# Pairwise bilinear interaction on one core: a quarter of the products summed over elements by VectorE in place of TensorE

## The chip, the core and the metric

One core of one Trainium2 chip. The metric is the device time of one execution in microseconds (us); the time before is the median of 3 runs. TensorE is called PE, VectorE DVE, ScalarE ACT, GpSimd POOL, SyncE SP.

## What is computed

2048 samples, 32 fields, embeddings of 64 floats (fp32 throughout). For every sample and each of the 496 pairs of fields a bilinear form with its own 64 x 64 matrix, then three dense layers:

```python
e = jnp.stack([tbl_0[ids[:, 0]], ..., tbl_31[ids[:, 31]]], axis=1)        # (2048, 32, 64)
row_idx, col_idx = np.triu_indices(32, k=1)
z = jnp.einsum('bpe,fpe,bpf->bp', e[:, row_idx], kernel, e[:, col_idx])   # (2048, 496)
h = jnp.concatenate([z, dense_ctx], axis=1)                               # (2048, 512)
h = jnp.maximum(h @ W_top1 + b_top1, 0.0)                                 # 512
h = jnp.maximum(h @ W_top2 + b_top2, 0.0)                                 # 256
y = h @ W_top3                                                            # 1
```

## The kernel before, in words

The samples go through in 4 chunks of 512. A chunk's embeddings are gathered by POOL (L202), one indirect DMA per field and 128 samples, 8 for a pair of fields, into a ring of 4 pairs. A "turn" on PE (L238) transposes a pair's rows into `side_ps`, so that elements lie in partitions and samples in columns; ACT copies it to `xt` (L363), a ring of 24 pairs: field 2q in partitions 0 to 63, field 2q+1 in 64 to 127.

The unit of work is the duo: for the field pairs s < q all four products of their fields. Its matmuls (L312, L313, each two instructions in fp32) have the kernel matrices as weights and the samples of pair q moving, half the rows of the array each, side by side, into one of 3 two-bank tiles `y_ps`. Four "special" duos a chunk hold the pairs inside field pairs (L315 to L318). DVE multiplies the 128 x 1024 result by x of pair s (L461) into one of 6 `products`. What is left is the sum over the 64 elements, which lie in partitions: PE does it by matmuls with a selector (L330), 4 column groups side by side, for two duos (a quad) at a time, collecting 16 quads in `sum_ps` before ACT copies the bank to `z_sb`. 124 duos and 62 quads make a chunk. The results of four banks, with 16 dense values put into the last by four DMAs, are the input of the dense layers ("layer1" four jobs, "layer2" two, "layer3" one; L250, L257, L264).

Turns and dense layers are side jobs: they share the one tile `side_ps`, so each waits until ACT has taken the one before. The order is written out by hand in `side_schedule`: the duos come in the order of q, after each duo number d with d % 4 == 1 the sums of the two quads before the last two duos, and side jobs just after such sums; the dense layers of a chunk run within the next one, and four times a chunk two jobs stand at one place. The last chunk's tower runs at the end (`last_tower`). The waits that pace PE and DVE:

```python
pe.wait_ge(duo_multiplied, g - Y_RING + 1)                # before the matmuls of duo g
pe.wait_ge(duo_multiplied, 2 * g + 2)                     # before the sum of quad g
dve.wait_ge(quad_summed, (g - PRODUCT_RING) // 2 + 1)     # before the multiply of duo g
```

Of the kernel before, what the change touches and what calls it, by code (L numbers as in the profile page):

```python
# [7 lines left out]
ALU = mybir.AluOpType  # L8
# [4 lines left out]
P = 128  # L13
# [4 lines left out]
ROW_RING = 4  # L18
XT_RING = 24
Y_RING = 3  # L20
PRODUCT_RING = 6
SPECIALS = PAIRS // 4


def duo_list():
# [12 lines left out]
DUO = duo_list()  # L38
DUOS = len(DUO)
QUADS = DUOS // 2  # L40
FIRST_DUO = {q: DUO.index(("block", 0, q)) for q in range(1, PAIRS)}
SPECIAL_DUO = {u: DUO.index(("special", u, None)) for u in range(SPECIALS)}

Z_QUADS = P // 8
Z_BANKS = -(-QUADS // Z_QUADS)
SUM_ROWS = 2 * (QUADS - (Z_BANKS - 1) * Z_QUADS)

PIECES = [(0, 4)] + [(d, d + 8) for d in range(4, DUOS, 8)]
# [14 lines left out]
def z_rows():  # L63
    rows, dense = [], 0
    for kb in range(Z_BANKS):
        for r in range(P):
            column_tile, s, half = r // 32, r % 32 // 2, r % 2
            quad = kb * Z_QUADS + s
            if quad < QUADS:
                duo = DUO[2 * quad + column_tile // 2]  # L70
                rows.append(tuple(sorted(field_pair(duo, column_tile % 2, half))))
            else:
                rows.append(dense)
                dense += 1
    return rows


def quads_after(d):


    return (d // 2 - 2, d // 2 - 1) if d % 4 == 1 else ()


def after_sums(d):

    return d - (d - 2) % 4


def side_schedule():

    before = {(c, d): [] for c in range(CHUNKS) for d in range(DUOS)}
    for c in range(CHUNKS):
        for q in range(PAIRS):
            if c == 0:
                at = 0 if q < 2 else FIRST_DUO[q] if q < 7 else after_sums(min(FIRST_DUO[q] - 4, 30 + 6 * (q - 8)))
                before[0, at].append(("turn", 0, q))
            elif q < 8:
                before[c - 1, after_sums(82 + 6 * q if c == 1 else 66 + 7 * q)].append(("turn", c, q))
            else:
                before[c, after_sums(6 + 7 * (q - 8))].append(("turn", c, q))  # L100
    for c in range(CHUNKS - 1):
        for n in range(4):
            before[c + 1, after_sums(10 + 6 * n)].append(("layer1", c, n))
        for n in range(2):
            before[c + 1, after_sums(38 + 8 * n)].append(("layer2", c, n))
        before[c + 1, after_sums(60)].append(("layer3", c, 0))
    after = [("layer1", CHUNKS - 1, n) for n in range(4)] + [("layer2", CHUNKS - 1, n) for n in range(2)]
    after.append(("layer3", CHUNKS - 1, 0))
    return before, after


SIDE_BEFORE, SIDE_AFTER = side_schedule()
SIDE_ORDER = [job for c in range(CHUNKS) for d in range(DUOS) for job in SIDE_BEFORE[c, d]] + SIDE_AFTER
# [3 lines left out]
def dlrm_tower(nc, ids, tables, pair_kernel, dense, w1, b1, w2, b2, w3, out):  # L117
    with ExitStack() as ctx:
# [9 lines left out]
        kernel_sb = sb("kernel_sb", [P, DUOS, 2 * E])  # L128
        xt = sb("xt", [P, XT_RING, N])
        special = sb("special", [P, 2, 2, N])  # L130
        rows = sb("rows", [P, ROW_RING, TILES, 2, E])
        products = sb("products", [P, PRODUCT_RING, 2, N])
        z_sb = sb("z_sb", [P, Z_BANKS, N])
# [7 lines left out]
        y_sb = sb("y_sb", [P, N])  # L141
# [8 lines left out]
        ids_landed = [sem(f"ids_landed{i}") for i in range(2)]  # L150
        rows_landed = [sem(f"rows_landed{i}") for i in range(ROW_RING)]
# [10 lines left out]
        duo_ready = sem("duo_ready")  # L162
        duo_multiplied = sem("duo_multiplied")
        quad_summed = sem("quad_summed")
        bank_kept = sem("bank_kept")
        out_written = sem("out_written")

        LAST_BANK = Z_BANKS - 1

        def x_of(c, q):  # L170
            return xt[:, (c * PAIRS + q) % XT_RING]

# [13 lines left out]
        def _(pool):  # L186
# [4 lines left out]
            for c in range(CHUNKS):  # L191
                if c < 2:
                    pool.wait_ge(ids_landed[c], 16)
                for q in range(PAIRS):
                    slot = q % ROW_RING
                    if c or q >= ROW_RING:
                        before = c * PAIRS + q - ROW_RING
                        pool.wait_ge(side_ready, SIDE["turn", before // PAIRS, before % PAIRS] + 1)
                    for h in range(2):
                        j = 2 * q + h  # L200
                        for t in range(TILES):
                            pool.indirect_dma_start(rows[:, slot, t, h, :], None, tables[j],  # L202
                                                    bass.IndirectOffsetOnAxis(ap=idx[:, c, t, j:j + 1], axis=0)
                                                    ).then_inc(rows_landed[slot], 16)

        @block.sync
        def _(sp):
# [8 lines left out]
            def place_dense(c):  # L216
                for g in range(4):
                    sp.dma_start(z_sb[32 * g + SUM_ROWS:32 * g + 32, LAST_BANK, :],
                                 dense[4 * g:4 * g + 4, c * N:c * N + N]).then_inc(dense_landed[c], 16)

            place_dense(0)
            for c in range(CHUNKS):
                if c + 1 < CHUNKS:
                    sp.wait_ge(side_ready, SIDE["layer1", c, 3] + 1)
                    place_dense(c + 1)
                sp.wait_ge(side_kept, SIDE["layer3", c, 0] + 1)
                sp.dma_start(out[:, c * N:c * N + N], y_sb[32 * c:32 * c + 1, :]).then_inc(out_written, 16)
# [3 lines left out]
        def _(pe):  # L231
            def turn(c, q):
                k = SIDE["turn", c, q]
                pe.wait_ge(rows_landed[q % ROW_RING], (c * (PAIRS // ROW_RING) + q // ROW_RING + 1) * 2 * TILES * 16)
                if k:
                    pe.wait_ge(side_kept, k)
                for t in range(TILES):
                    last = nc.tensor.transpose(side_ps[:, t * P:(t + 1) * P],  # L238
                                               rows[:, q % ROW_RING, t].rearrange("p h e -> p (h e)"), identity[:])
                last.then_inc(side_ready, 1)  # L240

            def layer1(c, n):
                if n == 0:
                    pe.wait_ge(bank_kept, banks_kept(c, LAST_BANK))
                    pe.wait_ge(dense_landed[c], 4 * 16)
# [3 lines left out]
                for kb in range(4):  # L249
                    last = nc.tensor.matmul(tower_bank(c, 1, n), w1_sb[:, kb, n * P:n * P + P], z_sb[:, kb, :],  # L250
# [17 lines left out]
            def last_tower(c):  # L268
                pe.wait_ge(side_kept, SIDE["layer1", c, 0])
                pe.wait_ge(bank_kept, banks_kept(c, LAST_BANK - 1))  # L270
                for n in range(4):
                    for kb in range(LAST_BANK):
                        nc.tensor.matmul(tower_bank(c, 1, n), w1_sb[:, kb, n * P:n * P + P], z_sb[:, kb, :],  # L273
                                         start=(kb == 0), stop=False)
                pe.wait_ge(bank_kept, banks_kept(c, LAST_BANK))
                pe.wait_ge(dense_landed[c], 4 * 16)
                for n in range(4):
                    nc.tensor.matmul(tower_bank(c, 1, n), w1_sb[:, LAST_BANK, n * P:n * P + P], z_sb[:, LAST_BANK, :],  # L278
# [14 lines left out]
            def side(job):  # L293
                kind, c, n = job
                if kind == "turn":
                    turn(c, n)
                elif kind == "layer1":
# [6 lines left out]
            def bilinear(c, d):  # L304
                g = c * DUOS + d
                if g >= Y_RING:
                    pe.wait_ge(duo_multiplied, g - Y_RING + 1)
                kind, s, q = DUO[d]
                y = y_ps[g % Y_RING]
                low, high = slice(0, E), slice(E, P)  # L310
                if kind == "block":
                    nc.tensor.matmul(y[:, 0, :], kernel_sb[low, d, :], x_of(c, q)[low, :], start=True, stop=True)  # L312
                    last = nc.tensor.matmul(y[:, 1, :], kernel_sb[high, d, :], x_of(c, q)[high, :], start=True, stop=True)  # L313
                else:
                    nc.tensor.matmul(y[low, 0, :], kernel_sb[low, d, low], x_of(c, 4 * s + 3)[low, :], start=True, stop=True)  # L315
                    nc.tensor.matmul(y[low, 1, :], kernel_sb[high, d, low], x_of(c, 4 * s)[high, :], start=True, stop=True)  # L316
                    nc.tensor.matmul(y[high, 0, :], kernel_sb[low, d, high], x_of(c, 4 * s + 2)[low, :], start=True, stop=True)  # L317
                    last = nc.tensor.matmul(y[high, 1, :], kernel_sb[high, d, high], x_of(c, 4 * s + 1)[high, :],  # L318
                                            start=True, stop=True)
                last.then_inc(duo_ready, 1)  # L320

            def add_up(c, quad):
                g = c * QUADS + quad
                pe.wait_ge(duo_multiplied, 2 * g + 2)
                kb, s = quad // Z_QUADS, quad % Z_QUADS
                if s == 0 and c * Z_BANKS + kb >= 1:
                    free = c * Z_BANKS + kb - 1
                    pe.wait_ge(bank_kept, banks_kept(free // Z_BANKS, free % Z_BANKS))
                for m in range(4):
                    last = nc.tensor.matmul(sum_ps[32 * m:32 * m + 32, :], selector[:, 30 - 2 * s:62 - 2 * s],  # L330
                                            products[:, (2 * g + m // 2) % PRODUCT_RING, m % 2, :],
                                            start=(s == 0), stop=(s == Z_QUADS - 1 or quad == QUADS - 1))
# [4 lines left out]
            for c in range(CHUNKS):  # L337
                stored, pieces = 0, 0
                for d in range(DUOS):
                    for job in SIDE_BEFORE[c, d]:  # L340
                        side(job)
                    kind, s, q = DUO[d]
                    need = SIDE["turn", c, q if kind == "block" else 4 * s + 3] + 1
                    if need > stored:
                        stored = need
                        pe.wait_ge(side_kept, stored)
                    if c == 0 and pieces < len(PIECES) and PIECES[pieces][0] == d:
                        pe.wait_ge(kernel_landed[pieces], 16)
                        pieces += 1
                    bilinear(c, d)  # L350
                    for quad in quads_after(d):
                        if quad >= 0:
                            add_up(c, quad)
                        elif c:
                            add_up(c - 1, QUADS + quad)
# [5 lines left out]
        def _(act):  # L361
# [3 lines left out]
            def store(c, q):  # L365
                k = SIDE["turn", c, q]
                if c * PAIRS + q >= XT_RING:
                    act.wait_ge(duo_multiplied, ((c * PAIRS + q - XT_RING) // PAIRS + 1) * DUOS)
# [17 lines left out]
            def keep3(c):  # L386
                k = SIDE["layer3", c, 0]
                act.wait_ge(side_ready, k + 1)
                copy(y_sb[32 * c:32 * c + 32, :], tower_bank(c, 3, 0)[32 * c:32 * c + 32, :]).then_inc(side_kept, 1)

            def keep(job):
                kind, c, n = job
                if kind == "turn":
                    store(c, n)
                elif kind == "layer1":
# [6 lines left out]
            def special_slots(c, u):  # L402
                n = c * SPECIALS + u
                if n >= 2:
# [102 lines left out]
```

## Time and profile before

| | |
|---|---|
| median of 3 runs | 896.94 us (896.54 to 897.68) |
| profiled execution: its time / its span | 896.94 / 894.2 us |
| PE busy | 831.9 us (93%) |
| DVE busy | 574.1 us (64%), 499 instructions |
| ACT busy | 114.3 us (13%) |
| POOL busy | 484.1 us (54%) |
| mean granted PE clock | 0.989 of full speed |

Busy times are of one profiled execution; PE's weight loads, which run beside its matmuls, are kept apart. In a row of the timeline "x8" merges neighbouring instructions of one kind; the time in brackets is the idle time of the engine before it and what ended it.

### The profile page before, as it was taken

Reading aid. Unit: us, or ns where it says so; the run is one execution under the profiler, and the core shown is the slowest. Engines: PE = TensorE matmul, PEld = TensorE weight load, DVE = VectorE, ACT = ScalarE, POOL = GpSimd, SP = SyncE. Lnnn points to the kernel's source line nnn. Section 1 sums busy time; section 2 is a strip of 40 time slices with the busy share of each in tenths; the row PEclk is TensorE's granted clock in tenths of the full one; section 3 lists DMA queues with packets and bytes.
Section 4 is the critical chain, followed back from the end, with each engine's and each line's share of the span. In section 5 each row is a group of like instructions: output and inputs, shape, how many; then the busy total and the mean of one; then the engine's idle time right before and its main releaser. Section 6 shows DMA issues by size and latency. Waiting matters only on the chain.

```text
span 894.2 us, 10971 instructions
## 1 busy us (share of the span) xinstructions
PE 831.9 (93%) x4496; PEld 293.4 (33%) x4496; DVE 574.1 (64%) x499; ACT 114.3 (13%) x185; POOL 484.1 (54%) x518
## 2 busy tenths in 40 slices
PE   0377999999899999999999999999999999999999
PEld 0122333333333333333333333333333333333323
DVE  0144778778666566787785466787775664788870
ACT  0011010100121011102111110200120210100112
POOL 6777777777777777477735555377746330000000
PEclk9988999999999999999999999999999999999999
DMA  9411111111111111011101111011111000000000
GB/s 340 156 27 26 28 27 27 27 28 27 26 27 26 29 28 26 17 27 26 27 13 21 21 19 22 13 28 25 27 18 22 14 14 1 1 1 1 1 1 0
DMA packets 19881, 27.64 MB, mean 31 GB/s; under 512 B 9012, under 2 KB 9268, under 8 KB 19704
## 3 DMA queue, kind: packets, MB, share of 16 engines
q0 software_dynamic: 16384, 16.81, 10.4%
q1 hardware_dynamic: 3448, 10.14, 3.1%
q8 instruction: 35, 0.57, 0.3%
q14 instruction: 14, 0.11, 0.0%
HBM read 26.91 MB, written 0.01 MB: 30 GB/s over the span
## 4 chain that ended last, share of the span: by engine, by line
PE 69%; POOL 22%; issue 7%; ACT 1%; DMA 0%; DVEq 0%; DVE 0%; ACTq 0%; POOLq 0%
PE y_ps L312 35%; POOL rows L202 22%; PE sum_ps L330 19%; PE side_ps L250 5%; PE side_ps L238 3%; PE side_ps L257 2%; PE y_ps L315 1%; PE y_ps L273 1%; ACT xt L363 1%; PE y_ps L283 1%; PE y_ps L313 1%; PE side_ps L264 1%; PE y_ps L278 0%; DMA rows<-tbl_dram,idx 0%; DMA idx<-ids_dram 0%
## 5 line engine op out<-in xcount | busy, mean ns | idle before, releaser
L461 DVE TENSOR_TENSOR products<-y_ps,xt 128x1024 f32<-128x1024 f32 x480 | 556.3, 1217 | 287.2 <-PE y_ps L313 287.0
L202 POOL DMA_INDIRECT rows<-tbl_dram,idx x512 | 483.4, 944 | 239.7 <-issue 151.7
L312 PE MATMUL y_ps<-xt,kernel_sb 64*128 64x512 f32 x960 | 459.0, 616 | 4.1 <-ACT xt L363 4.1
L313 PE MATMUL y_ps<-xt,kernel_sb 64*128 64x512 f32 x960 | 459.2, 617 | 0.0
L312 PEld LDWEIGHTS y_ps<-xt,kernel_sb 64*128 64x128 f32 x960 | 168.6, 190 | 256.7 <-issue 145.0
L330 PE MATMUL sum_ps<-products,selector 128*32 128x512 f32 x1984 | 238.8, 598 | 0.7 <-DVE products L461 0.7
L313 PEld LDWEIGHTS y_ps<-xt,kernel_sb 64*128 64x128 f32 x960 | 168.6, 190 | 0.0
L330 PEld LDWEIGHTS sum_ps<-products,selector 128*32 128x32 f32 x1984 | 51.6, 109 | 170.4 <-DVE products L461 94.2
L363 ACT ACTIVATE xt<-side_ps 128x512 f32<-128x512 f32 x64 | 38.2, 598 | 442.9 <-PE side_ps L238 442.8
L238 PE MATMUL side_ps<-identity,rows 128*128 128x128 f32 x256 | 44.2, 298 | 46.1 <-DMA rows<-tbl_dram,idx 46.1
L238 PEld LDWEIGHTS side_ps<-identity,rows 128*128 128x128 f32 x256 | 28.3, 146 | 100.2 <-issue 60.1
L250 PE MATMUL side_ps<-z_sb,w_sb 128*128 128x512 f32 x96 | 44.3, 604 | 4.8 <-ACT xt L363 4.8
L363 ACT ACTIVATE z_sb<-sum_ps 28x512 f32<-28x512 f32 (+1 forms) x28 | 16.6, 592 | 208.3 <-PE sum_ps L330 208.0
L363 ACT ACTIVATE special<-xt 64x512 f32<-64x512 f32 x64 | 40.1, 627 | 1.6
L250 PEld LDWEIGHTS side_ps<-z_sb,w_sb 128*128 128x128 f32 x96 | 17.2, 189 | 28.3 <-issue 25.4
L257 PE MATMUL side_ps<-h_sb,w_sb 128*128 128x512 f32 x48 | 22.2, 605 | 4.5 <-ACT xt L363 4.5
L461 DVE TENSOR_TENSOR products<-y_ps,special 128x1024 f32<-128x1024 f32 x16 | 19.5, 1217 | 6.0 <-issue 4.3
L377 ACT ACTIVATE h_sb<-side_ps,b_sb 128x512 f32<-128x512 f32 x12 | 8.2, 687 | 73.6 <-PE side_ps L250 73.6
L317 PE MATMUL y_ps<-xt,kernel_sb 64*64 64x512 f32 x32 | 17.1, 615 | 0.0
L315 PE MATMUL y_ps<-xt,kernel_sb 64*64 64x512 f32 x32 | 17.1, 615 | 0.0
L316 PE MATMUL y_ps<-xt,kernel_sb 64*64 64x512 f32 x32 | 17.1, 614 | 0.0
L318 PE MATMUL y_ps<-xt,kernel_sb 64*64 64x512 f32 x32 | 17.1, 614 | 0.0
(29 smaller groups left out, 73.1 us busy)
## 6 DMA issues: line engine op xcount, KB each, us to landing
rows<-tbl_dram,idx POOLq DMA_INDIRECT x512, 2.4
kernel_sb<-pair_kernel_dram SPq DMA_DIRECT2D x15, 512.0 KB, 11.1
w_sb<-w_dram SPq DMA_DIRECT2D x1, 1024.0 KB, 18.2
w_sb<-w_dram SPq DMA_DIRECT2D x1, 512.0 KB, 17.5
kernel_sb<-pair_kernel_dram SPq DMA_DIRECT2D x1, 256.0 KB, 2.8
z_sb<-dense_dram SPq DMA_DIRECT2D x16, 8.0 KB
idx<-ids_dram SPq DMA_DIRECT2D x1, 192.0 KB, 6.9
idx<-ids_dram SPq DMA_DIRECT2D x1, 64.0 KB, 1.9
```

Source lines behind the costliest of these rows:

```text
L202: pool.indirect_dma_start(rows[:, slot, t, h, :], None, tables[j], bass.IndirectOffsetOnAxis(ap=idx[:, c, t, j:j + 1], axis=0)).then_inc(r ...
L238: last = nc.tensor.transpose(side_ps[:, t * P:(t + 1) * P], rows[:, q % ROW_RING, t].rearrange("p h e -> p (h e)"), identity[:])
L250: last = nc.tensor.matmul(tower_bank(c, 1, n), w1_sb[:, kb, n * P:n * P + P], z_sb[:, kb, :], start=(kb == 0), stop=(kb == 3))
L257: last = nc.tensor.matmul(tower_bank(c, 2, n), w2_sb[:, kb, n * P:n * P + P], h1_sb[:, kb, :], start=(kb == 0), stop=(kb == 3))
L312: nc.tensor.matmul(y[:, 0, :], kernel_sb[low, d, :], x_of(c, q)[low, :], start=True, stop=True)
L313: last = nc.tensor.matmul(y[:, 1, :], kernel_sb[high, d, :], x_of(c, q)[high, :], start=True, stop=True)
L315: nc.tensor.matmul(y[low, 0, :], kernel_sb[low, d, low], x_of(c, 4 * s + 3)[low, :], start=True, stop=True)
L316: nc.tensor.matmul(y[low, 1, :], kernel_sb[high, d, low], x_of(c, 4 * s)[high, :], start=True, stop=True)
L317: nc.tensor.matmul(y[high, 0, :], kernel_sb[low, d, high], x_of(c, 4 * s + 2)[low, :], start=True, stop=True)
L330: last = nc.tensor.matmul(sum_ps[32 * m:32 * m + 32, :], selector[:, 30 - 2 * s:62 - 2 * s], products[:, (2 * g + m // 2) % PRODUCT_RING, ...
L363: return nc.scalar.activation(dst, src, ACT.Copy)
L461: nc.vector.tensor_tensor(products[:, g % PRODUCT_RING], y_ps[g % Y_RING][:], by, ALU.mult).then_inc(duo_multiplied, 1)
```

## The change

Of the 124 duos, the 28 with s < 4 and q in (4, 6, 8, 9, 10, 12, 13) are replaced by 28 batches. A batch (q, t) takes 128 samples of pair q as weights and the kernel matrices of the four duos (s = 0 to 3) moving: its result has samples in partitions and, for both fields of pair q, 8 x 64 elements in columns. DVE multiplies it by the gathered rows of fields 0 to 7, which are kept untransposed (`kept_rows`, two chunks deep), into one of 2 `batch_products`, and after the multiply of the next unit adds up the 64 elements of each group in one `tensor_reduce` (1024 elements to 16 per partition). The 16 results go to `z_batch`, to which dense is now loaded with one DMA; one more turn per chunk ("turn_batch") makes it the fourth bank `z_turned`. Duos and batches are units: 96 duos, 28 batches, 48 quads a chunk, three banks. Sums come after the second duo of four as before, or after the batch that follows it. Side jobs may stand before the sums of a place (odd keys) or after them (even keys), one at each place. `PRODUCT_RING` goes from 6 to 5, `special` from two buffers to one, the ring of gathered rows to 3.

The order in chunks 1 to 3 as it comes out (d duo, s special duo, b batch, S two quads' sums, T a turn, TB the batch turn, L1, L2, L3 layer jobs; a line ends at its sums):

```
dd TB S          T5 dddd L1 S       sdbddb T6 S        T7 ddbddb L1 S
ddbddb L1 S      T8 ddbdsb S        T9 ddddb L1 S      T10 ddddb S
L2 ddbddb S      T11 ddddb L2 S     ddbddb L3 S        ddddb S
T12 ddsdb S      ddbddb S           T13 ddddb S        ddbddb S
T14 ddddb S      ddddb S            ddbddb S           ddddb S
T15 ddbdd S      dddd S             T0 ddsd T1 S       T2 dddd T3 S, T4 dd
```

T0 to T4 on the last lines are of the next chunk, and chunk 3 has there only TB, before the sums of "ddsd". In chunk 0 there are no L jobs; from T10 on its order is: T10 ddddb, ddbddb, T11 ddddb, ddbddb, ddddb, T12 ddsdb, ddbddb and on as above.

```diff
-PRODUCT_RING = 6
+PRODUCT_RING = 5
+BATCH_RING = 2
+BATCH_Q = (4, 6, 8, 9, 10, 12, 13)
...
+        units.append(duo)
+        due = BATCHES * (a // 4 + 1) // (DUOS // 4 - 4)
+        if a % 2 and waiting and placed < due:
+            units.append(waiting.pop(0))
...
+    places = [key for g in range(CHUNKS * UNITS - 1) if SUMS_AFTER[g] for key in (2 * g + 1, 2 * g + 2)]
...
             def bilinear(c, p):
-                    pe.wait_ge(duo_multiplied, g - Y_RING + 1)
+                    pe.wait_ge(unit_multiplied, g - Y_RING + 1)
...
+                else:
+                    d, samples = PLACE["block", 0, s], slice(q * P, q * P + P)
+                    nc.tensor.matmul(y[:, 0, :], x_of(c, s)[low, samples],
+                                     kernel_sb[low, d:d + KEPT, :].rearrange("p d f -> p (d f)"), start=True, stop=True)
+                    last = nc.tensor.matmul(y[:, 1, :], x_of(c, s)[high, samples],
+                                            kernel_sb[high, d:d + KEPT, :].rearrange("p d f -> p (d f)"),
+                                            start=True, stop=True)
...
+                bilinear(c, p)
+                for job in SIDE_AT[2 * g + 1]:
+                    side(job)
+                for of, quad in SUMS_AFTER[g]:
+                    add_up(of, quad)
...
+            def sum_batch(n):
...
+                dve.wait_ge(unit_multiplied, batch_unit(n) + 1)
+                nc.vector.tensor_reduce(z_batch[:, t, 16 * block:16 * block + 16],
+                                        batch_products[:, n % BATCH_RING].rearrange("p b i e -> p (b i) e"),
+                                        mybir.AxisListType.X, ALU.add).then_inc(batch_summed, 1)
...
+                dve.wait_ge(unit_ready, g + 1)
+                if kind == "batch":
+                    if batches >= BATCH_RING:
+                        dve.wait_ge(batch_summed, batches - BATCH_RING + 1)
+                    by = kept_rows[:, c % 2, q].rearrange("p i e -> p (i e)").unsqueeze(1).to_broadcast([P, 2, N])
...
+                    if duos >= PRODUCT_RING:
+                        dve.wait_ge(quad_summed, (duos - PRODUCT_RING) // 2 + 1)
...
+                nc.vector.tensor_tensor(into, y[:], by, ALU.mult).then_inc(unit_multiplied, 1)
+                if p and UNIT[p - 1][0] == "batch":
+                    sum_batch(batches - 1)
```

## Rows read from the trace of the kernel before

**Rows 1.** The page, busy us of each engine, share of the span, instructions.
```profile
PE 831.9 (93%) x4496; PEld 293.4 (33%) x4496; DVE 574.1 (64%) x499; ACT 114.3 (13%) x185; POOL 484.1 (54%) x518
```
**Rows 2.** The page, costliest groups: line, engine, form, count | busy us, mean ns | idle before.
```profile
L461 DVE TENSOR_TENSOR products<-y_ps,xt 128x1024 f32<-128x1024 f32 x480 | 556.3, 1217 | 287.2 <-PE y_ps L313 287.0
...
L312 PE MATMUL y_ps<-xt,kernel_sb 64*128 64x512 f32 x960 | 459.0, 616 | 4.1 <-ACT xt L363 4.1
...
L330 PE MATMUL sum_ps<-products,selector 128*32 128x512 f32 x1984 | 238.8, 598 | 0.7 <-DVE products L461 0.7
```
**Rows 3.** The chain that ended last, a layer 1 job in two chunks: start, us.
```profile
473.04 3.67 PE side_ps L250 x8
...
680.55 3.67 PE side_ps L250 x8
```
**Rows 4.** Timeline of PE in chunk 3: start us, us, instruction.
```profile
807.53 1.92 PE L330 MATMUL sum_ps<-products,selector 128*32 128x512 f32 x16
809.39 0.69 PE L312 MATMUL y_ps<-xt,kernel_sb 64*128 64x512 f32 x1
...
810.35 0.59 PE L312 MATMUL y_ps<-xt,kernel_sb 64*128 64x512 f32 x1
...
812.07 0.59 PE L312 MATMUL y_ps<-xt,kernel_sb 64*128 64x512 f32 x1
...
813.02 1.92 PE L330 MATMUL sum_ps<-products,selector 128*32 128x512 f32 x16
```
**Rows 5.** Timeline of DVE over the same stretch.
```profile
806.25 3.48 DVE L461 TENSOR_TENSOR products<-y_ps,xt 128x1024 f32<-128x1024 f32 x3
810.63 4.62 DVE L461 TENSOR_TENSOR products<-y_ps,xt 128x1024 f32<-128x1024 f32 x4 [0.91 <-PE y_ps L313]
```
**Rows 6.** Timeline of PE, sums and the side jobs between them.
```profile
264.03 0.66 PE L238 MATMUL side_ps<-identity,rows 128*128 128x128 f32 x4 [0.40 <-DMA rows<-tbl_dram,idx]
...
265.53 3.67 PE L250 MATMUL side_ps<-z_sb,w_sb 128*128 128x512 f32 x8 [0.84 <-ACT xt L363]
...
272.76 1.92 PE L330 MATMUL sum_ps<-products,selector 128*32 128x512 f32 x16
...
281.88 1.92 PE L330 MATMUL sum_ps<-products,selector 128*32 128x512 f32 x16
...
357.46 1.92 PE L330 MATMUL sum_ps<-products,selector 128*32 128x512 f32 x16
...
364.65 1.93 PE L330 MATMUL sum_ps<-products,selector 128*32 128x512 f32 x16
...
388.13 1.92 PE L330 MATMUL sum_ps<-products,selector 128*32 128x512 f32 x16
...
394.25 1.92 PE L330 MATMUL sum_ps<-products,selector 128*32 128x512 f32 x16
```
**Rows 7.** Timeline of PE, turns that waited for rows, first sum of chunk 1.
```profile
84.15 0.66 PE L238 MATMUL side_ps<-identity,rows 128*128 128x128 f32 x4 [3.90 <-DMA rows<-tbl_dram,idx]
...
244.07 0.66 PE L238 MATMUL side_ps<-identity,rows 128*128 128x128 f32 x4 [1.92 <-DMA rows<-tbl_dram,idx]
...
249.98 1.93 PE L330 MATMUL sum_ps<-products,selector 128*32 128x512 f32 x16
```
**Rows 8.** Timeline of PE and DVE, the last sums.
```profile
862.78 1.93 PE L330 MATMUL sum_ps<-products,selector 128*32 128x512 f32 x16
...
865.88 2.36 DVE L461 TENSOR_TENSOR products<-y_ps,xt 128x1024 f32<-128x1024 f32 x2 [0.87 <-PE y_ps L313]
...
866.55 1.06 PE L330 MATMUL sum_ps<-products,selector 128*32 128x512 f32 x8
...
868.29 1.06 PE L330 MATMUL sum_ps<-products,selector 128*32 128x512 f32 x8 [0.67 <-DVE products L461]
```
**Rows 9.** Stretches: us, busy us (count) of PE, PEld, DVE, ACT, POOL, PE clock, DMA share, GB/s.
```profile
80.00:100.00 20.00, 16.11 (x86) 6.28 (x84) 10.10 (x10) 3.71 (x6) 15.12 (x17) 0.91 0.15 27
100.00:150.00 50.00, 50.00 (x302) 17.46 (x302) 39.90 (x36) 6.06 (x10) 37.82 (x41) 1.00 0.16 27
```

More of the change, by code:

```diff
@@ L63, in z_rows @@
 def z_rows():
-    rows, dense = [], 0
+    rows = []
     for kb in range(Z_BANKS):
@@ L67, in z_rows @@
             column_tile, s, half = r // 32, r % 32 // 2, r % 2
[L68 to L71, printed above, removed]
-            else:
[L73 to L100, printed above, removed]
+            duo = DUO[2 * (kb * Z_QUADS + s) + column_tile // 2]
@@ new lines, in z_rows, with sum_schedule @@
+            rows.append(tuple(sorted(field_pair(duo, column_tile % 2, half))))
+    for q in BATCH_Q:
+        rows += [(i, 2 * q + bank) for bank in range(2) for i in range(2 * KEPT)]
+    return rows + list(range(DENSE))
+def sum_schedule():
+    after, summed = {g: [] for g in range(CHUNKS * UNITS)}, 0
+    waits = [FIRST_UNIT[q] - 1 for q in range(2, 8)]
+    for c in range(CHUNKS):
+        for p in range(UNITS):
+            duos = sum(at <= p for at in DUO_AT)
+            upto = summed
+            if c == 0 and p in waits:
+                upto = duos // 2
+            elif duos % 4 == 2 and (p == UNITS - 1 or UNIT[p + 1][0] != "batch"):
+                upto = c * QUADS + duos // 2 - 1
+            after[c * UNITS + p] = [divmod(quad, QUADS) for quad in range(summed, upto)]
+            summed = max(summed, upto)
+    return after
@@ new lines, with side_schedule @@
+SUMS_AFTER = sum_schedule()
+def side_schedule():
+    at = {key: [] for key in range(2 * CHUNKS * UNITS)}
+    places = [key for g in range(CHUNKS * UNITS - 1) if SUMS_AFTER[g] for key in (2 * g + 1, 2 * g + 2)]
+    for c in range(CHUNKS):
+        after = (c + 1) * UNITS if c < CHUNKS - 1 else c * UNITS + LAST_BATCH + 8
+        at[min(key for key in places if key > 2 * after)].append(("turn_batch", c, 0))
+    later = 2 * CHUNKS * UNITS
+    for c in reversed(range(CHUNKS)):
+        for q in reversed(range(PAIRS)):
+            if c == 0 and q < 8:
+                key = 2 * FIRST_UNIT[q] if q else 0
+            else:
+                last = 2 * (c * UNITS + FIRST_UNIT[max(q, 1)] - 2)
+                key = later = max(key for key in places if key <= last and key < later and not at[key])
+            at[key].insert(0, ("turn", c, q))
@@ L101, in side_schedule @@
     for c in range(CHUNKS - 1):
+        free = [key for key in places if key > 2 * (c + 1) * UNITS + 8 and not at[key]]
         for n in range(4):
-            before[c + 1, after_sums(10 + 6 * n)].append(("layer1", c, n))
+            at[free[2 * n]].append(("layer1", c, n))
         for n in range(2):
-            before[c + 1, after_sums(38 + 8 * n)].append(("layer2", c, n))
-        before[c + 1, after_sums(60)].append(("layer3", c, 0))
+            at[free[8 + 2 * n]].append(("layer2", c, n))
@@ L107, in side_schedule @@
+        at[free[12]].append(("layer3", c, 0))
     after = [("layer1", CHUNKS - 1, n) for n in range(4)] + [("layer2", CHUNKS - 1, n) for n in range(2)]
     after.append(("layer3", CHUNKS - 1, 0))
-    return before, after
-SIDE_BEFORE, SIDE_AFTER = side_schedule()
-SIDE_ORDER = [job for c in range(CHUNKS) for d in range(DUOS) for job in SIDE_BEFORE[c, d]] + SIDE_AFTER
+    return at, after
+SIDE_AT, SIDE_AFTER = side_schedule()
+SIDE_ORDER = [job for key in range(2 * CHUNKS * UNITS) for job in SIDE_AT[key]] + SIDE_AFTER
@@ L150, in dlrm_tower @@
         ids_landed = [sem(f"ids_landed{i}") for i in range(2)]
+        kept_landed = [sem(f"kept_landed{q}") for q in range(KEPT)]
         rows_landed = [sem(f"rows_landed{i}") for i in range(ROW_RING)]
@@ L336, in _ @@
             pe.wait_ge(selector_made, 2)
[L337 to L355, printed above, removed]
+            stored, pieces = 0, 0
+            for g in range(CHUNKS * UNITS):
+                c, p = divmod(g, UNITS)
+                for job in SIDE_AT[2 * g]:
+                    side(job)
+                need = SIDE["turn", c, top_pair(UNIT[p])] + 1
+                if need > stored:
+                    stored = need
+                    pe.wait_ge(side_kept, stored)
+                kind, s, q = UNIT[p]
+                place = PLACE["block", 0, s] + KEPT - 1 if kind == "batch" else PLACE[UNIT[p]]
+                while c == 0 and pieces < len(PIECES) and PIECES[pieces][0] <= place:
+                    pe.wait_ge(kernel_landed[pieces], 16)
+                    pieces += 1
+                bilinear(c, p)
+                for job in SIDE_AT[2 * g + 1]:
+                    side(job)
+                for of, quad in SUMS_AFTER[g]:
+                    add_up(of, quad)
             add_up(CHUNKS - 1, QUADS - 2)
@@ L414, in copy_bank @@
+                copy(special[high, 0, :], x_of(c, 4 * u + 2)[high, :]).then_inc(special_kept, 1)
+                copy(special[low, 0, :], x_of(c, 4 * u + 3)[high, :]).then_inc(special_kept, 1)
             def copy_bank(c, kb):
-                act.wait_ge(quad_summed, c * QUADS + min(Z_QUADS * (kb + 1), QUADS))
-                if c and kb == 0:
+                act.wait_ge(quad_summed, c * QUADS + Z_QUADS * (kb + 1))
+                if c and kb == 1:
                     act.wait_ge(side_ready, SIDE["layer1", c - 1, 3] + 1)
-                if kb < LAST_BANK:
-                    copy(z_sb[:, kb, :], sum_ps[:]).then_inc(bank_kept, 1)
-                else:
-                    for g in range(4):
-                        part = slice(32 * g, 32 * g + SUM_ROWS)
-                        copy(z_sb[part, kb, :], sum_ps[part, :]).then_inc(bank_kept, 1)
@@ L439, in _ @@
-            copy_bank(CHUNKS - 1, LAST_BANK)
+                copy(z_of(c, kb), sum_ps[:]).then_inc(bank_kept, 1)
+            for g in range(CHUNKS * UNITS):
+                for job in SIDE_AT[2 * g] + SIDE_AT[2 * g + 1]:
+                    keep(job)
+                    if job[0] == "turn" and job[2] % 4 == 3:
+                        special_slots(job[1], job[2] // 4)
+                for of, quad in SUMS_AFTER[g]:
+                    if quad % Z_QUADS == Z_QUADS - 1:
+                        copy_bank(of, quad // Z_QUADS)
```

219 lines of the change are left out of this document (132 added, 87 removed).

## The prediction

> **What bounds the kernel now.** I read the page's busy shares first: PE is busy 93% of the span and DVE 64% [rows 1]. The costliest groups say of what: 496 multiplies of 1.22 us on DVE (480 in the row shown, 16 more for the special duos), and on PE the duo and sum matmuls [rows 2]. The chain of waits repeats with the chunk: the same layer 1 job stands at 473.04 and at 680.55, so a chunk takes 207.5 us [rows 3]. The timeline of PE gives the unit of the rest. Between two sums without a side job lie 5.49 us (807.53 to 813.02): the sum of two quads 1.86, the first duo 0.96, three more at 0.86 (810.35 to 812.07 is two duos), and 0.09 before the next sum [rows 4]. I call this a pattern; a chunk is 31 of them. In the same pattern DVE does four multiplies in 4.62 us and then waits 0.91 us for PE [rows 5]. Its pitch in a row is (4.62 - 1.22)/3 = 1.134 us. So PE sets the pace and DVE has 0.9 us of room in 5.49.
>
> Side jobs lengthen a pattern: a turn makes it 6.12 us, so 0.63; layer 3 makes it 7.19, so 1.70; a layer 1 or 2 job makes it 9.12, so 3.63. Where two jobs stand together, PE waits 0.84 us for ACT between them [rows 6]; that happens four times a chunk. Check: 31 x 5.49 + 16 x 0.63 + 6 x 3.63 + 1.70 + 4 x 0.84 = 207.1, measured 207.5. Until about 250 us the gathers also count: turn 7 of chunk 0 and turn 7 of chunk 1 wait for rows at 84.15 and 244.07, 16 pairs apart, so one pair comes every 10.0 us; the first sum of chunk 1 starts at 249.98 [rows 7].
>
> **The change, part by part.** PE: 96 duos and 28 batches a chunk have the same matmul shapes as 124 duos, so 0.86 each. 62 quads become 48, 24 patterns in place of 31, and 7 x (5.49 - 4 x 0.86) = 14.3 us a chunk go. One more turn (the batch sums) adds 0.63, and no two jobs stand at one place any more, which saves 3.4. PE's own work falls from 207.5 to about 190 us a chunk. The last bank's four small copies become one and dense comes in one DMA instead of four a chunk: nothing on the path, since 12 matmuls of layer 1 run before they are needed. The 512 gathers stay; POOL's new waits (ring of 3, kept rows doubled): pair q+3 comes up 20 us after pair q has landed, in chunk 0 turn 12 alone is nearly that late, and the next chunk's first four pairs need no turn; I cost them at nothing, covered by rows that land ahead of their turns, and at 10 us a pair if that cover were gone. SP's two new waits have only dense and out behind them, needed a chunk later.
>
> DVE: 28 reductions a chunk of 1024 elements per partition. The trace has no reduction; the nearest row is the multiply of as many elements. I take its pitch, R = 1.134. Ends: half of it (one operand instead of two), 0.57; twice it, 2.27. The Trainium skill (VectorE: DVE Perf Modes, the perf-mode tier table) has `tensor_reduce` at 1x only; by that page's cycle table an estimate is (58 + 1024)/0.96 GHz = 1.127 us, which would move the sum by under 1 us. No row here shows it.
>
> By shares this looks good: DVE 172 us of work a chunk against PE's 190. But the batches aren't even. From the listed order, a chunk has 5 patterns without a batch, 10 with one and 9 with two. DVE's work is 4.54, 5 x 1.134 + R = 6.80 and 6 x 1.134 + 2R = 9.07 us; PE's without side jobs 5.49, 6.35 and 7.21. With batches DVE is the longer, and the queues between the two are short (3 y banks, 5 products). So I walk a pattern through.
>
> One batch: units A B C D b, then the sum. PE may start b only when B is multiplied (three y banks). PRODUCT_RING 5 in place of 6 now makes D's multiply wait for the first quad of this pattern's sum, which PE does after b. From the start of B's multiply: 1.22 for it, 0.05 to PE (a multiply ends at 868.24, the sum starts at 868.29), 0.95 for b (812.07 to 813.02 [rows 4]), 1.06 for one quad, 0.11 back to DVE: 3.39 us until D can start [rows 8]. DVE has B and C, 2.27 us, and stands still for 1.12. After D come b, the next A, the reduction, the next B: 4 x 1.134. Period 3.39 + 4.54 = 7.93 us, with neither engine full. Two batches: A B b C D b: now b is held by the first b, and DVE has b, C and a reduction, 3.40, in the 3.39. Period 9.07, DVE full. The last batch of a chunk lies before C, where it makes D wait for nothing. In all, going from step to step costs 7.93 into a one-batch pattern and 9.07 into a two-batch one.
>
> Side jobs in such stretches: one that stands before the sum delays D in full, since DVE is held by that sum. One after it delays the next A: A would be ready 2.22 + 1.86 + 1.24 = 5.32 us after B's start (1.24 is from 809.39 to 810.63 [rows 4, 5]), and DVE is free for it at 3.39 + 2.27 = 5.66, so 0.34 us are hidden; a turn costs 0.3 and a layer job 3.3. Per chunk, before the sum: three layer 1 and one layer 2 (3.63 each), layer 3 (1.70), turn 6 (0.63); after it: a layer 2 (3.3) and nine turns at 0.3. Together 22.9 us.
>
> The sum of a chunk, from its first sum to the next chunk's: first two patterns and the way into the batches 15.1 (9.8 with turn 5 and a layer 1 job, then 5.4 to the first batch's multiply); eight steps into two-batch patterns 72.6; ten into one-batch patterns 79.3; side jobs 22.9; from the last of them to the sum of the next pattern 7.9; three patterns without a batch, with two turns each (once a turn and the batch turn), 3 x 6.75 = 20.2. That is 218.0, against 207.5. Chunk 0: gathers pace it to turn 10, which lands at 84.15 + 3 x 10 = 114; from there 4.1 to the first reference, 5 x 9.07 + 8 x 7.93 + 1.5 for turns, 7.9 and 3 x 6.75: first sum of chunk 1 at 256.5, against 249.98 [rows 7], so 6.5 later. Chunks 1 and 2: 2 x 218. Chunk 3 to its last full pattern's sum: 218 - 6.75 - 4 x 0.63 + 0.63 = 209.4. Then the old tail, 894.2 - 862.78 = 31.4 [rows 8]. Span 256.5 + 436 + 209.4 + 31.4 = 933.3; the profiled run's time was 896.94 with a span of 894.2 (and equals the median), so 2.7 outside: **936 us**, 4.4% slower. A difference under about 0.2% can't be told from none by a measurement of this kernel.
>
> **The rivals.** (1) Faster, the opposite sign: the wait of D for the sum doesn't bind and DVE runs through side jobs. Each pattern then takes the larger of the two works, side jobs counted to PE: 35.5 us for the five without a batch (side jobs 8.0 of it), 87.5 for the nine with two, 76.5 for the ten with one, 199.5 a chunk, 18.5 less than mine, 10 less in chunk 0, so 936 - 3 x 18.5 - 10 = 870. Its place is 35 one-batch patterns (1.12 us each) and 18 layer jobs; it decides if PE starts b more than 1.1 us earlier than B's multiply allows, or products go free sooner. For it: shares (DVE 690 us of work in 896). Against: the rings are written so. If even the unevenness between patterns were smoothed, PE's 190 a chunk would give 832; three y banks can't do that. Together 0.13. (2) The reduction is cheap, at the low end 0.57. One reduction in each of 71 steps is on the path (19 a chunk and 14 in chunk 0), so 936 - 71 x 0.57 = 896: no change. One operand instead of two speaks for it; a reduction reads every element as the multiply does against. 0.08. Beside it: the same page gives single-source fp32 copies in SBUF two elements a cycle, but excludes the reduction. (3) Slower still: the reduction near 2.27, where both of a two-batch pattern count (103 in all), 936 + 103 x 1.134 = 1053; or PE's clock. In 80 to 100 us, with PE busy 16.1 of 20 us, the granted clock was 0.91, at full work 1.00 [rows 9]. One-batch patterns have PE busy 6.35 of 7.93, the same share, though in gaps of 1 us and not of 4. Matmuls at 0.91 all through add 0.1 x (0.95 + 1.06) to a step, 71 x 0.2 = 14 us, so 950. Together 0.12. (4) My forecast, 0.67. That fewer sums are issued, and 112 reductions, is plain from the code; that the change doesn't act isn't a case.
>
> **The numbers.** The forecast's own range, from the terms rounded and R from 1.05 to 1.25, is 928 to 948. To hold 8 in 10 I go down to 892, which takes in the cheap reduction, and up to 962, which takes in the clock. Faster: rival 1 and half of the cheap reductions, 0.16. Same 0.03. Slower 0.81.
>
> **What would show it.** DVE busy about 700 us; in the stretches with batches DVE waits for the sum (L330's line) about 1.1 us before the second duo after a one-batch pair; sums 9.1 and 7.9 us apart there, 5.5 where no batch is; chunks 218 us apart by their layer 1 jobs; PE idle a tenth of the chunk, waiting for DVE. A reduction far from 1.13 us, sums nearer than 7.5 us in one-batch patterns, or chunks under 207 us would prove me wrong.

## The result and the profile after

The changed kernel takes 940.16 us (940.15 to 940.34, 4 runs) against 897.01 us before in the same comparison: ratio 1.048, 95% interval 1.046 to 1.050. Forecast: 936, 4.4% slower, with a range from 892 to 962.

The page after (the busy shares and two groups of the multiplies and reductions; columns as in [rows 1] and [rows 2]):

```profile
PE 812.6 (87%) x4064; PEld 272.7 (29%) x4064; DVE 701.8 (75%) x611; ACT 107.7 (11%) x173; POOL 484.0 (52%) x518
...
L569 DVE TENSOR_TENSOR products<-y_ps,xt 128x1024 f32<-128x1024 f32 x368 | 442.8, 1219 | 206.2 <-PE sum_ps L421 115.2
...
L543 DVE TENSOR_REDUCE z_batch<-batch_products 128x16 f32<-128x1024 f32 x112 | 135.4, 1209 | 0.0
```

PE has less to do than in [rows 1] and is less busy in a longer span; no engine is full. The reduction lasts 1.21 us, as the multiply does. New is what DVE waits for. Before, it waited almost only for the matmuls of a duo (L313 in [rows 2]); now the largest of its waits in the changed kernel (us in total, times, longest) is the one for the sum, L421:

```profile
DVE products L569 <- PE sum_ps L421: 115.2, 62, 4.8
DVE products L569 <- PE y_ps L396: 87.8, 28, 30.3
```

The timeline of DVE over two one-batch patterns of chunk 1 shows the walk (A, B, C and D are the four duos of a pattern in order, as in the prediction; a step is the way from one pattern's sum to the next one's):

```profile
415.97 2.34 DVE L569 TENSOR_TENSOR products<-y_ps,xt 128x1024 f32<-128x1024 f32 x2
419.50 1.23 DVE L569 TENSOR_TENSOR products<-y_ps,xt 128x1024 f32<-128x1024 f32 x1 [1.19 <-PE sum_ps L421]
420.64 1.22 DVE L569 TENSOR_TENSOR batch_products<-y_ps,kept_rows 128x1024 f32<-128x1024 f32 x1
421.78 1.22 DVE L569 TENSOR_TENSOR products<-y_ps,xt 128x1024 f32<-128x1024 f32 x1
422.91 1.21 DVE L543 TENSOR_REDUCE z_batch<-batch_products 128x16 f32<-128x1024 f32 x1
424.03 2.35 DVE L569 TENSOR_TENSOR products<-y_ps,xt 128x1024 f32<-128x1024 f32 x2
427.56 1.22 DVE L569 TENSOR_TENSOR products<-y_ps,xt 128x1024 f32<-128x1024 f32 x1 [1.18 <-PE sum_ps L421]
```

B and C in a row, then 1.19 us of waiting, then D, the batch, A, the reduction, and B again. The timeline of PE in the same stretch has the other half: the batch's matmuls start only when B is multiplied, and the sum follows.

```profile
417.24 0.69 PE L407 MATMUL y_ps<-kernel_sb,xt 64*128 64x512 f32 x1 [1.01 <-DVE products L569]
...
418.30 1.92 PE L421 MATMUL sum_ps<-products,selector 128*32 128x512 f32 x16
...
426.36 1.93 PE L421 MATMUL sum_ps<-products,selector 128*32 128x512 f32 x16
```

From B's start to D's it is 419.50 - 415.97 = 3.53 us, forecast 3.39; the period is 426.36 - 418.30 = 8.06, forecast 7.93. The 0.14 more are in two places: the first matmul pair of the batch, which stands behind a wait, starts 0.53 us before the next where one that follows on takes 0.43, so 1.06 from the batch to the sum (0.95 in the forecast's addition), and 1.20 from the sum's start to D (1.17).

A layer job that stands before the sum costs DVE its full time, here layer 1 in a two-batch pattern (PE, then DVE):

```profile
285.88 2.84 PE L330 MATMUL side_ps<-z_sb,w_sb 128*128 128x512 f32 x6
288.56 1.02 PE L330 MATMUL side_ps<-z_turned,w_sb 128*128 128x512 f32 x2
289.51 1.92 PE L421 MATMUL sum_ps<-products,selector 128*32 128x512 f32 x16
```
```profile
285.81 1.21 DVE L543 TENSOR_REDUCE z_batch<-batch_products 128x16 f32<-128x1024 f32 x1
290.71 1.22 DVE L569 TENSOR_TENSOR products<-y_ps,xt 128x1024 f32<-128x1024 f32 x1 [3.69 <-PE sum_ps L421]
```

The stages add up as forecast, a little longer each. The first sum of chunk 1 starts at 258.63 (forecast 256.5); the layer 1 job that answers to [rows 3] comes again after 219.2 and 218.8 us (forecast 218):

```profile
264.78 3.63 PE side_ps L330 x8
...
483.96 3.63 PE side_ps L330 x8
...
702.78 3.63 PE side_ps L330 x8
```

In windows (columns as in [rows 9]) DVE is busy 175 of 219 us, PE 200, with a granted clock of 1.00; the last full sum stands at 907.03 and the span ends at 938.4, 31.4 us on, as before.

```profile
264.78:483.96 219.18, 200.36 (x1017) 67.19 (x1017) 175.33 (x153) 26.59 (x43) 120.80 (x129) 1.00 0.10 20
483.96:702.78 218.82, 199.99 (x1018) 67.31 (x1017) 175.32 (x153) 26.60 (x43) 120.80 (x129) 1.00 0.10 20
```

### The profile page after: what moved, and what is told of

Its sections match the earlier page's. It is cut to its first block, busy times and chain, and to the rows that moved or that the text cites. A ratio compares the mean times of both kernels' runs of the same rounds, so it can differ in the third digit from the quotient of the medians.

```text
span 938.4 us, 10192 instructions
## 1 busy us (share of the span) xinstructions
PE 812.6 (87%) x4064; PEld 272.7 (29%) x4064; DVE 701.8 (75%) x611; ACT 107.7 (11%) x173; POOL 484.0 (52%) x518
## 4 chain that ended last, share of the span: by engine, by line
PE 54%; DVE 23%; issue 17%; POOL 5%; DVEq 0%; DMA 0%; ACT 0%
PE y_ps L395 15%; PE sum_ps L421 15%; DVE products L569 11%; PE y_ps L407 8%; DVE z_batch L543 7%; DVE batch_products L569 5%; PE side_ps L330 5%; PE side_ps L311 4%; POOL kept_rows L273 3%; PE side_ps L337 2%; POOL rows L273 2%; PE y_ps L399 1%; PE y_ps L354 1%; PE y_ps L363 1%; PE side_ps L344 1%
## 5 line engine op out<-in xcount | busy, mean ns | idle before, releaser
L569 DVE TENSOR_TENSOR products<-y_ps,xt 128x1024 f32<-128x1024 f32 x368 | 442.8, 1219 | 206.2 <-PE sum_ps L421 115.2
L273 POOL DMA_INDIRECT rows<-tbl_dram,idx x384 | 362.4, 944 | 300.4 <-PE side_ps L311 189.2
L395 PE MATMUL y_ps<-xt,kernel_sb 64*128 64x512 f32 x736 | 372.6, 625 | 37.9 <-DVE products L569 33.3
L396 PE MATMUL y_ps<-xt,kernel_sb 64*128 64x512 f32 x736 | 372.7, 626 | 0.0
L395 PEld LDWEIGHTS y_ps<-xt,kernel_sb 64*128 64x128 f32 x736 | 124.1, 188 | 244.6 <-DVE products L569 126.3
L421 PE MATMUL sum_ps<-products,selector 128*32 128x512 f32 x1536 | 190.9, 601 | 3.7 <-DVE products L569 3.7
L407 PE MATMUL y_ps<-kernel_sb,xt 64*128 64x512 f32 x224 | 123.2, 630 | 36.5 <-DVE products L569 36.3
L273 POOL DMA_INDIRECT kept_rows<-tbl_dram,idx x128 | 120.9, 945 | 40.2 <-issue 38.4
L569 DVE TENSOR_TENSOR batch_products<-y_ps,kept_rows 128x1024 f32<-128x1024 f32 x112 | 136.1, 1215 | 0.5 <-PE y_ps L409 0.5
L543 DVE TENSOR_REDUCE z_batch<-batch_products 128x16 f32<-128x1024 f32 x112 | 135.4, 1209 | 0.0
L396 PEld LDWEIGHTS y_ps<-xt,kernel_sb 64*128 64x128 f32 x736 | 123.5, 188 | 0.0
L409 PE MATMUL y_ps<-kernel_sb,xt 64*128 64x512 f32 x224 | 123.3, 630 | 0.0
L421 PEld LDWEIGHTS sum_ps<-products,selector 128*32 128x32 f32 x1536 | 40.6, 109 | 128.5 <-issue 115.8
L407 PEld LDWEIGHTS y_ps<-kernel_sb,xt 64*128 64x128 f32 x224 | 34.9, 186 | 118.3 <-DVE products L569 66.1
L409 PEld LDWEIGHTS y_ps<-kernel_sb,xt 64*128 64x128 f32 x224 | 34.8, 186 | 0.0
```

What stands on the lines that cost most here:

```text
L273: pool.indirect_dma_start(rows_of(c, q, t)[:, h, :], None, tables[j], bass.IndirectOffsetOnAxis(ap=idx[:, c, t, j:j + 1], axis=0)).then_in ...
L407: nc.tensor.matmul(y[:, 0, :], x_of(c, s)[low, samples], kernel_sb[low, d:d + KEPT, :].rearrange("p d f -> p (d f)"), start=True, stop=True)
L409: last = nc.tensor.matmul(y[:, 1, :], x_of(c, s)[high, samples], kernel_sb[high, d:d + KEPT, :].rearrange("p d f -> p (d f)"), start=True, ...
L543: nc.vector.tensor_reduce(z_batch[:, t, 16 * block:16 * block + 16], batch_products[:, n % BATCH_RING].rearrange("p b i e -> p (b i) e"), ...
L569: nc.vector.tensor_tensor(into, y[:], by, ALU.mult).then_inc(unit_multiplied, 1)
```

## The experiments

The first four kernels ran first on a chip where everything took about a quarter longer, the kernel before too (1124.09 us); the profiled runs there have a mean granted clock of 0.88 to 0.92, and in e4's trace PE waits 74.6 us in 30 stops, up to 24.4 us at a time, for nothing that the profile shows. Their ratios to the kernel before were 1.064 (e1), 1.045 (e2), 1.034 (e3) and 0.996 (e4). The order of the four is that of the theory, but their microseconds can't be set against a kernel that takes 897. All four ran again on another chip, and those runs are read here.

**e1, the ring of products.**
```diff
-PRODUCT_RING = 5
+PRODUCT_RING = 6
```


> The changed kernel with PRODUCT_RING 6 again, nothing else. My theory (a step is the walk from the multiply that frees a y bank, over the batch's matmuls and the sum, to the next multiply): D no longer waits for this sum, but the next A then waits for its matmuls, which PE starts only after the same sum, 5.32 us after B's start against 5.66 before. So only 0.34 us go, and only in steps without a turn after the sum: seven a chunk in chunks 1 to 3 and six in chunk 0, 9 us in all: 940 becomes 931. The idle time of DVE moves from 'waits for the sum' (L421) to 'waits for the duo' (L396). Rival (the smaller ring is the whole stall): 35 one-batch patterns lose 1.12 us each, about 901.

> The kernel of e1 again (PRODUCT_RING 6 in the changed kernel), since the first time all kernels, the one before too, ran a quarter slower. Same expectations: my theory 931 (9 us less than the changed kernel, DVE's idle time moves from the sum to the duo), the rival (the smaller ring is the whole stall) 901.

Measured: 927.21 us (926.64 to 927.35) against 896.86 before, ratio 1.033 (1.031 to 1.035): 13 us less than the changed kernel, not 39. The waits show the move: no wait for the sum is left, and the wait for the duo has grown from 87.8 to 187.4 us.

```profile
DVE products L569 <- PE y_ps L396: 187.4, 86, 30.3
```

In the timeline of DVE the one-batch pattern without a turn has its wait one place later, before A, and is 7.62 us long (412.17 to 419.79 between the sums) where I had 7.59:

```profile
413.23 1.22 DVE L569 TENSOR_TENSOR batch_products<-y_ps,kept_rows 128x1024 f32<-128x1024 f32 x1
415.20 1.23 DVE L569 TENSOR_TENSOR products<-y_ps,xt 128x1024 f32<-128x1024 f32 x1 [0.75 <-PE y_ps L396]
```

So the smaller ring costs 13 us of the 43, and most of what it seems to cost in the waits (115 us) is only named after it. I had 9 from 0.34 us in each of 27 steps. In the rows each of these steps is about 0.43 shorter: 8.06 becomes 7.62, and 9.19 into a two-batch pattern (sums at 426.36 and 435.55) becomes 8.76 (419.79 and 428.55). Five steps out of a two-batch pattern are 0.15 shorter as well, since with the real 3.53 D waits 0.13 there too.

**e2, the price of the reduction.**
```diff
-                                        batch_products[:, n % BATCH_RING].rearrange("p b i e -> p (b i) e"),
+                                        batch_products[:, n % BATCH_RING].rearrange("p b i e -> p (b i) e")[:, :, :E // 2],
```


> The changed kernel, each reduction over 32 of the 64 elements (the other half of the sum is left out). My theory: the reduction goes from 1.13 to about 0.60 us, and one of them in each of 71 steps is on the path, the second of a two-batch pattern is hidden by the wait of D for the sum: 940 - 71 x 0.53 = 902. If DVE's work alone bounded, all 112 count: 940 - 112 x 0.53 = 881. If PE alone bounded: 940.

> The kernel of e2 again (each reduction over 32 of 64 elements, half of each sum left out). My theory: one reduction in each of 71 steps is on the path, 940 - 71 x 0.53 = 902; DVE's work alone bounds: 881; PE alone: 940.

Measured: 902.34 us (902.27 to 902.43), ratio 1.006 (1.003 to 1.008). The reduction's row says 0.68 us in place of 1.21, 0.53 less:

```profile
L543 DVE TENSOR_REDUCE z_batch<-batch_products 128x16 f32<-128x512 f32 x112 | 75.7, 676 | 0.0
```

37.8 us for 112 reductions that are 0.53 shorter is 71 of them, the count that the walk gives; the other 41 were behind the wait for the sum. The total fits better than its parts: 8.6 us in chunk 0 are 16 reductions (the walk has 14), and about 9.75 in each later chunk are 18.3 (19), since the last of them saves only 0.17. Even with reductions half as long the kernel is still 5.5 us behind the one before.

**e3, the place of the single batch.**
```diff
-        due = BATCHES * (a // 4 + 1) // (DUOS // 4 - 4)
+        due = BATCHES * ((a + 2) // 4 + 1) // (DUOS // 4 - 4)
```


> The changed kernel, single batches placed after the second duo of a pattern (ddbdd) where they stood after the fourth (ddddb); the same 28 batches in about the same stretch. My theory: the batch's multiply and reduction now lie between B and D, so D doesn't wait for the sum, and a one-batch pattern costs DVE's own 6.80 us in place of 7.93. By the same walk a chunk comes to 208 us in place of 219, the first sum of chunk 1 comes 10 us earlier: about 897. Rival (DVE's amount of work bounds, not its order): the same 940.

> The kernel of e3 again (single batches after the second duo of a pattern). My theory: D no longer waits for the sum, one-batch patterns without a side job 6.8 us apart in place of 8.1, about 897. Rival (the amount of DVE's work bounds, not its order): 940.

Measured: 897.61 us (896.40 to 898.05), ratio 1.000 (0.999 to 1.001): the same instructions in another order are 42.6 us faster, practically all of the loss. The chunk is 208.1 us (first sums at 248.98 and 457.11), 208 expected, and the first sum of chunk 1 comes 9.7 us earlier, 10 expected. The sums of PE around a one-batch pattern that follows another, with a turn in it, are 7.09 us apart; the changed kernel has 8.22 for the like (443.61 to 451.83, turn at 445.47):

```profile
394.00 1.92 PE L421 MATMUL sum_ps<-products,selector 128*32 128x512 f32 x16
395.86 0.66 PE L311 MATMUL side_ps<-identity,rows 128*128 128x128 f32 x4
401.09 1.92 PE L421 MATMUL sum_ps<-products,selector 128*32 128x512 f32 x16
```

In this stretch DVE passes the place of D without a wait for the sum (batch, C, reduction, then D and the next A and B in one row). It is not gone everywhere: elsewhere in this kernel 66.4 us of such waits are left of 115.2.

```profile
401.02 1.21 DVE L569 TENSOR_TENSOR products<-y_ps,xt 128x1024 f32<-128x1024 f32 x1
402.15 1.21 DVE L543 TENSOR_REDUCE z_batch<-batch_products 128x16 f32<-128x1024 f32 x1
403.28 3.47 DVE L569 TENSOR_TENSOR products<-y_ps,xt 128x1024 f32<-128x1024 f32 x3
```
```profile
DVE products L569 <- PE sum_ps L421: 66.4, 36, 3.8
```

The rule that places the batches also shifts some of them: a middle chunk of e3 has 10 patterns with two batches and 8 with one, where the changed kernel has 9 and 10.

**e4, a part alone: side jobs apart, in the kernel before.**
```diff
-            before[c + 1, after_sums(10 + 6 * n)].append(("layer1", c, n))
+            before[c + 1, (10, 14, 22, 30)[n]].append(("layer1", c, n))
         for n in range(2):
-            before[c + 1, after_sums(38 + 8 * n)].append(("layer2", c, n))
+            before[c + 1, (42, 50)[n]].append(("layer2", c, n))
```


> The kernel before with one part of the change alone: side jobs spread so that three of the four places a chunk with two jobs have one. Each such place cost PE 0.84 us of waiting for ACT: 9 x 0.84 = 7.6 us less than the kernel before, 889.4. Rival (the wait only moves to the next turn): 897.

> The kernel of e4 again (the kernel before, three of four double places a chunk split up). My theory: 9 x 0.84 = 7.6 us less than the kernel before, 889.3. Rival (the wait only moves): 897.

Measured: 891.44 us (888.98 to 892.23) against 898.32, ratio 0.991 (0.989 to 0.993): 6.9 us less, 7.6 expected. PE's waits for ACT before layer jobs fall from 9.3 us in 12 places to 2.5 in 3, which is the whole gain. This part of the change is a gain by itself.

**e5, side jobs in pieces, where PE waits anyway.** On e3, with `PRODUCT_RING = 6`: each matmul of a layer job is a piece of its own, and pieces and turns stand before the third or fourth duo.
```diff
-                for kb in range(4):
-                    last = nc.tensor.matmul(tower_bank(c, 1, n), w1_sb[:, kb, n * P:n * P + P], z_of(c, kb),
-                                            start=(kb == 0), stop=(kb == 3))
-                last.then_inc(side_ready, 1)
+                kb = part
+                last = nc.tensor.matmul(tower_bank(c, 1, n), w1_sb[:, kb, n * P:n * P + P], z_of(c, kb),
+                                        start=(kb == 0), stop=(kb == 3))
+                if part == 3:
+                    last.then_inc(side_ready, 1)
...
-                for job in SIDE_AT[2 * g]:
-                    side(job)
+                for job, part in PARTS_AT[2 * g]:
+                    side(job, part)
```


> e3's order with PRODUCT_RING 6, and the side jobs no longer next to the sums in the stretches with batches: each layer job is cut into its four (layer 3: two) matmuls of 0.86 us, which stand one by one before the third or fourth duo of a pattern, as do the turns. My theory: there PE would wait for a y bank anyway (1.9 us in a two-batch pattern), so a piece delays neither the sum nor the next A. A chunk then comes to PE's own work, 190 us and about 0.15 more for each of 26 pieces (the change of the array's rows, 0.10 and 0.09 by the timeline before), some 195 against e3's 208; 860 in all, faster than the kernel before. Rival (what a side job costs doesn't depend on its place): as e3, 897.

Measured: 879.46 us (879.39 to 881.08), ratio 0.981 (0.978 to 0.983): faster than both kernels, by 18 of the 37 us that I expected from e3. A chunk is 200.7 us (sums of PE, the same one of chunks 1 and 2):

```profile
249.65 1.92 PE L488 MATMUL sum_ps<-products,selector 128*32 128x512 f32 x16
...
450.35 1.92 PE L488 MATMUL sum_ps<-products,selector 128*32 128x512 f32 x16
```

The step that missed is the price of a piece. A pattern with one batch and one piece, and one with two and two:

```profile
353.84 1.92 PE L488 MATMUL sum_ps<-products,selector 128*32 128x512 f32 x16
359.33 1.12 PE L392 MATMUL side_ps<-z_sb,w_sb 128*128 128x512 f32 x2
361.47 1.92 PE L488 MATMUL sum_ps<-products,selector 128*32 128x512 f32 x16
366.10 1.12 PE L392 MATMUL side_ps<-z_sb,w_sb 128*128 128x512 f32 x2
368.21 1.13 PE L392 MATMUL side_ps<-z_sb,w_sb 128*128 128x512 f32 x2
371.18 1.92 PE L488 MATMUL sum_ps<-products,selector 128*32 128x512 f32 x16
```

7.63 - 6.35 = 1.28 and (9.71 - 7.21)/2 = 1.25 us for 0.86 us of matmuls: between duos a piece costs 0.4 more, where I had 0.15. 26 x 0.25 = 6.5 us a chunk on top of 195 comes to 201.5, near the 200.7; that the price of the pieces is the whole difference is argued from this, since turns between duos cost more too (0.79 in place of 0.63 in the pattern from 371.18 to 379.57). The Trainium skill (TensorEngine Tiling (Array Packing), Key Properties) says that a change of the tiling mode drains the engine. These rows agree in that the two changes around a piece cost about 0.4 us together; whether a drain is the reason they don't show.

e5 differs from e3 in three things at once, the ring, the size of the jobs and their place. What each gives of the 18 us wasn't measured.

**e6, halves in place of quarters.**
```diff
-            parts[key].append((current, size - left))
-            left -= 1
+            for _ in range(2):
+                parts[key].append((current, size - left))
+                left -= 1
```


> e5 with the layer jobs in halves (two matmuls, 1.71 us) where they were in quarters, one half before the fourth duo of a pattern, and some turns next to a sum again. In e5 two pieces made a two-batch pattern 9.71 us where PE's work without them is 7.21, so a piece of 0.86 costs PE 0.39 more for changing the array's rows twice. My theory: PE is the bound there, half as many changes for the layer jobs are 12 x 0.39 = 4.7 us a chunk, some of it given back where a half (2.1 us) is more than PE would have waited: 3 us a chunk, 870. Rival (DVE bounds in e5): 879.

Measured: 873.85 us (871.98 to 873.95), ratio 0.972 (0.970 to 0.975) to the kernel before, 898.32 there: 5.6 us less than e5, 9 expected. The two ran in different comparisons; by their ratios (0.981 and 0.972) e6 gains about 7 us. The places of the halves and of some turns changed with their size, so the gain isn't that of the size alone. In the profile PE is now busy nearly all the time in this stretch of 200 us, 199.49 of it. That hides waits under 0.16 us, since a matmul's row lasts 0.59 us where the next starts after 0.43:

```profile
250.00:450.00 200.00, 199.49 (x1040) 69.46 (x1032) 175.80 (x155) 27.79 (x45) 120.81 (x128) 1.00 0.12 22
```

It is the fastest version made here, 2.8% under the kernel before and 7% under the changed one, with the change's own arithmetic and no instruction fewer.

## Why the prediction was right

- **The direction and the size**: the sum of the walk was 933.3 us of span, measured 938.4. Of the 5.1 missing, 2.1 are in chunk 0, 2.0 in chunks 1 and 2, 1.0 in chunk 3. In chunk 0, 1.1 of them are the later start of turn 10. The rest is the way of 3.39 us to D, which is 3.53: steps of 8.06 and 9.19 us where I had 7.93 and 9.07, partly taken back where a turn follows the sum. Outside the span lie 1.75 us, not 2.7, which brought the forecast of 936 about 1 us nearer by chance.
- **The reduction at the multiply's pitch**: shown. In the timeline a multiply follows the one before it after 1.14 us, a reduction the multiply before it after 1.13 us, and the next multiply the reduction after 1.12. Rival 2 (0.57) falls. That about 71 of 112 are on the path is what e2 gives in total.
- **The wait of D for the sum**: shown by the 1.19 us row, by e3, which takes the wait away in the stretch of single batches by another order and is 42.6 us faster, and by e1 as far as its 13 us go. Rival 1 (DVE runs through) falls for this order. The sentence "PRODUCT_RING 5 in place of 6 now makes D's multiply wait for the first quad of this pattern's sum" was true but named less than the cause: with six products A waits 0.75 us for its matmuls in place of D's 1.19. What costs is that the sum, and all behind it on PE, stands behind a batch that stands behind B.
- **Side jobs**: before the sum 3.6 us in full, as the 3.69 row has it. A turn after the sum costs 8.22 - 8.06 = 0.16 us, not 0.3: D's longer wait hides more of it. e5 and e6, with other places and sizes, are faster than e3, which fits a cost by place but doesn't show it alone. What share of the 43 us the side jobs' places have in the changed kernel, with all else left, wasn't tried alone.
- **Gathers pace chunk 0 to turn 10, at 114**: the number is near, the reason isn't the one given, and that is luck. Turn 10 starts at 115.08, but turns 6 to 10 no longer wait for rows; the steps of PE and DVE, 8.2 to 9.4 us long with batches in them, set the pace there, little less than the 10.0 us of a pair's gathers. In e2, where the steps are shorter, turn 10 does wait for rows again (at 114.08, after 2.28 us).
- **PE's clock** (rival 3): 1.00 in both windows above, though PE waits 19 us in 219. Its waits are near 1 us each. Only early in chunk 0 is it lower than before: 0.65 from 47 to 70 us, where PE is busy 13.0 of 23 us and waits 9.3 for rows, against 0.80 in the kernel before; from 90 us on it is 1.00 in both.
- **PE's own work**: put at about 190 us a chunk, never measured as such. PE is busy 200 of 219 us, and those 200 contain short waits that the rows don't show as idle, so the term stays open. The forecast's sum doesn't use it.
- **The expected gain**: it existed. PE is busy 812.6 us in place of 831.9, and e4 shows the part from side jobs apart. In the changed kernel's order it is given back at DVE, which has no room for two batches in a pattern, and at the wait for the sum.

## What to carry to other kernels

When work moves from the full engine to the one with room, compare the two per period of the loop and not per run, and then walk one period through the rings: which buffer lets each engine start, and what stands in order in front of the instruction that frees it. With rings of three and five buffers, the order of equal work was worth 43 us here, as much as the whole change cost. Long side jobs are worth trying where the engine waits for a buffer anyway, in pieces that fit the wait but not smaller: here each pair of changes of the array's shape around a piece cost 0.4 us.

## What was not expected

A first matmul pair after a wait for DVE takes 0.10 us longer than one that follows on (0.53 to 0.43); the first pair after a sum or a turn does too (446.06 to 446.59 behind the turn at 445.47). A lone 128-row matmul of 0.86 us between 64-row ones costs 1.25 to 1.28 us. And a wait that the profile puts at 115 us in total, DVE's for the sum, was worth 13 us when its buffers were enlarged, because the next instruction then waited for work behind the same sum.
